# Feature tile padded to 68 columns, low part of the fc2 product padded to 36 rows, and new engine orders in a two-layer attention kernel

## The reference

```
norm_X = layernorm(ctx) ; norm_F = layernorm(L0 output)
attended = softmax(norm_F @ norm_X.T / 16) @ norm_X
h = gelu(attended @ fc1_w.T + fc1_b)            # 4 features
cross = h @ fc2_w.T + fc2_b
self_att = softmax(norm_cross @ norm_cross.T / 16) @ norm_cross
out = norm_F + gamma2 * (cross + gamma1 * self_att)
```

## Time and profile before

| what | value |
|---|---|
| median of 3 runs | 1124.83 us (1122.71 to 1127.54) |
| the profiled execution's own time | 1123.86 us |
| its span, first to last instruction | 1122.1 us |
| mean granted TensorE clock | 0.945 of full |
| busy: PE / weight loads / DVE / ACT / POOL | 999.5 / 820.9 / 672.6 / 623.4 / 249.0 us |

### The profile page before, as it was taken

One profiled execution on the slowest core, in us unless ns is written; L12 is line 12 of the kernel. 1 busy time (PEld: TensorE's weight loads), 2 busy tenths in 40 slices (PEclk: granted clock), 3 DMA queues, 4 the chain that ended last, 5 costly groups with the idle time before them and its releaser, 6 DMA issues.

```text
span 1122.1 us, 22714 instructions
## 1 busy us (share of the span) xinstructions
PE 999.5 (89%) x8556; PEld 820.9 (73%) x8556; DVE 672.6 (60%) x1509; ACT 623.4 (56%) x1318; POOL 249.0 (22%) x306
## 2 busy tenths in 40 slices
PE   2576889899999999999999999999999999989764
PEld 1455677778788787878787787878887878777652
DVE  3624364758576675758485856667575848565542
ACT  4243446474756665665647465756567574845332
POOL 4000011112213131413132221213141312231332
PEclk9676789999999999999999999999999999999975
DMA  5221202110211212121112112121212111110000
GB/s 172 93 77 38 82 24 69 65 53 33 69 61 58 73 48 81 47 74 49 54 47 75 39 58 72 49 82 48 82 48 67 53 52 43 50 37 17 10 10 9
DMA packets 68868, 63.65 MB, mean 57 GB/s; under 512 B 17156, under 2 KB 64173, under 8 KB 68784
## 3 DMA queue, kind: packets, MB, share of 16 engines
q1 hardware_dynamic: 68784, 62.50, 17.3%
HBM read 16.18 MB, written 4.19 MB: 18 GB/s over the span
## 4 chain that ended last, share of the span: by engine, by line
PE 71%; DVE 13%; ACT 6%; issue 6%; DMA 2%; POOL 1%; SPq 1%; ACTq 0%; DVEq 0%; POOLq 0%
PE mring L928 16%; PE ring L928 15%; PE down_ps L1071 7%; PE od L1021 7%; DVE mx_sa L773 6%; PE ring L1007 5%; PE ring L987 4%; PE mring L1135 3%; PE ring L1033 2%; ACT probs L631 2%; PE ring L936 2%; PE mring L1081 2%; PE ring L1041 1%; PE mring L1098 1%; DVE xn_a L746 1%
## 5 line engine op out<-in xcount | busy, mean ns | idle before, releaser
L631 ACT ACTIVATE probs<-ring 128x1024 f32<-128x1024 f32 (+1 forms) x192 | 190.6, 1023 | 24.0 <-PE ring L1007 22.3
L502 POOL TENSOR_TENSOR hidT_lo<-hid,hidT_hi 128x256 fp32r<-128x256 f32 x128 | 93.9, 739 | 457.4 <-ACT hidT_hi L660 457.4
L773 DVE TENSOR_REDUCE mx_sa<-ring 128x4 f32<-128x1024 f32 x128 | 152.8, 1219 | 14.8 <-PE ring L987 14.8
L815 DVE SCALAR_TENSOR_TENSOR hid<-hid,mring 128x256 f32<-128x256 f32 x128 | 53.1, 415 | 84.9 <-ACT hid L652 84.8
L778 DVE TENSOR_REDUCE mx_ca<-ring 128x4 f32<-128x308 f32 x128 | 55.4, 475 | 78.2 <-PE ring L987 77.4
L652 ACT ACTIVATE hid<-mring 128x256 f32<-128x256 f32 x128 | 48.7, 380 | 83.2 <-PE mring L928 83.2
L987 PE MATMUL ring<-pk_sa 63*128 63x256 f32 x512 | 67.9, 347 | 27.7 <-DVE mx_sa L773 15.7
L987 PEld LDWEIGHTS ring<-pk_sa 63*128 63x128 f32 x512 | 41.3, 199 | 51.2 <-DVE mx_sa L773 16.0
L1071 PE MATMUL down_ps<-down_hi,hidT_hi 128*128 128x256 f32 x256 | 77.2, 302 | 0.0
L1021 PE MATMUL od<-probs,vz_sa 128*32 128x256 f32 x1024 | 76.8, 400 | 0.1
L1071 PE MATMUL down_ps<-down_lo,hidT_hi 128*128 128x256 f32 x256 | 72.5, 283 | 0.0
(11 more groups left out here) (235 smaller groups left out, 2645.0 us busy)
## 6 DMA issues: line engine op xcount, KB each, us to landing
pk_sa<-qkT SPq DMA_DIRECT2D x96, 256.0 KB, 2.6
qpk_ca<-qkT SPq DMA_DIRECT2D x48, 256.0 KB, 2.6
x_sb<-x SPq DMA_DIRECT2D x16, 256.0 KB, 2.7
x_res<-x SPq DMA_DIRECT2D x16, 256.0 KB, 2.9
out<-o_sb SPq DMA_DIRECT2D x16, 256.0 KB, 2.2
kpk_ca<-qkT SPq DMA_DIRECT2D x48, 78.0 KB, 2.3
ctx_sb<-ctx SPq DMA_DIRECT2D x16, 77.0 KB
ctx_l<-ctx SPq DMA_DIRECT2D x16, 77.0 KB
```

The source lines that it names most:

```text
L502: nc.gpsimd.tensor_tensor(hidT[1][:, m % HID, :], hid[:, m % 2, :], hidT[0][:, m % HID, :].bitcast(F32), ALU.subtract).then_inc(S["hidlo"] ...
L631: nc.scalar.activation(granule(g, tag)[0:rows_, i0:i0 + 2, :, :].rearrange("p i h t -> p h i t"), ring_tile(("E", tag, k))[0:rows_].rearra ...
L773: nc.vector.tensor_reduce(mx[tag][:, :, :, k].rearrange("p q h -> p h q"), ps[:].rearrange("p h (q t) -> p h q t", t=T), AX_X, ALU.max).th ...
L815: nc.vector.scalar_tensor_tensor(out=hid[:, m % 2, :], in0=hid[:, m % 2, :], scalar=1.0, in1=ps[:, 0:T], op0=ALU.add, op1=ALU.mult).then_i ...
```

## The change

`fc2_lo` gets the 36 rows of `fc2_hi`, its added rows zero, and the low product of `f2` runs over all 36 rows of `g_r`. `xf` gets 68 columns (`HALF + FC`, 64 + 4), the last 64 zero, and `h4` writes 68 PSUM rows, of which four are read as before. DVE clears both tiles once at the start; PE and DVE wait for five instead of three such fills. The five lists in `ORDER` are replaced; the same steps stand in them.

```
-        fc2_lo = sb("fc2_lo", [FC + 1, D], F32R)
+        fc2_lo = sb("fc2_lo", [LO_AT + FC, D], F32R)
-        xf = sb("xf", [SKV, FC])
+        xf = sb("xf", [SKV, HALF + FC])
...
-                nc.scalar.activation(xf[:], mring_tile(("sc",))[...], ACT.Copy)
+                nc.scalar.activation(xf[:, 0:FC], mring_tile(("sc",))[...], ACT.Copy)
...
+            nc.vector.memset(fc2_lo[:].bitcast(F32), 0.0).then_inc(s_vset, 1)
+            nc.vector.memset(xf[:], 0.0).then_inc(s_vset, 1)
+            dve.wait_ge(s_vset, 5)
...
-            nc.vector.tensor_tensor(fc2_lo[:], ...)
+            nc.vector.tensor_tensor(fc2_lo[0:FC + 1], ...)
...
-            pe.wait_ge(s_vset, 3)
+            pe.wait_ge(s_vset, 5)
...
-                mm(ps[0:FC, 0:T], xf[:], lpT, start=True, stop=True)
+                mm(ps[0:HALF + FC, 0:T], xf[:], lpT, start=True, stop=True)
...
-                    last = mm(ps[...], g_r[0:FC + 1, q * P:(q + 1) * P], fc2_lo[:], ...)
+                    last = mm(ps[...], g_r[:, q * P:(q + 1) * P], fc2_lo[:], ...)
```

The list of PE before and after:

```
-        dnp.2@-2 qk.sa@1 dnp.3@-2 dnp.4@-2 E.ca.0@-1 pv.sa.3@0 E.ca.1@-1 E.ca.2@-1 gu.7@-2 nCT@-3 oT.sa@0 E.ca.3@-1 pv.ca.0@-1 s2@-3 cT.ca@0 aT.sa@0
-        pv.ca.1@-1 v.ca@0 nXT@-2 oT.ca@-1 wo.sa@0 dnp.5@-2 S.sa.0@1 aT.ca@-1 dnp.6@-2 dnp.7@-2 S.sa.1@1 wo.ca@-1 S.sa.2@1 p2T@-3 S.sa.3@1 S.sa.4@1 pv2@-3
-        S.sa.5@1 T.mlp@-1 v.sa@1 S.sa.6@1 S.sa.7@1 gu.0@-1 T.ca@0 gu.1@-1 maxT.sa@1 qk.ca@0 gu.2@-1 dnp.0@-1 E.sa.0@1 E.sa.1@1 gu.3@-1 nFT@-2 E.sa.2@1
-        E.sa.3@1 pv.sa.0@1 sc@-2 E.sa.4@1 gu.4@-1 E.sa.5@1 S.ca.0@0 pv.sa.1@1 gu.5@-1 S.ca.1@0 E.sa.6@1 dnp.1@-1 pT@-2 E.sa.7@1 S.ca.2@0 h4@-2 pv.sa.2@1
-        S.ca.3@0 T.sa@2 gu.6@-1 maxT.ca@0 f2@-2
+        qk.sa@1 pv.sa.2@0 pv.sa.3@0 E.ca.0@-1 E.ca.1@-1 gu.7@-2 oT.sa@0 E.ca.2@-1 pv.ca.0@-1 nCT@-3 cT.ca@0 aT.sa@0 dnp.4@-2 E.ca.3@-1 dnp.5@-2 wo.sa@0
+        S.sa.0@1 pv.ca.1@-1 v.ca@0 oT.ca@-1 s2@-3 aT.ca@-1 S.sa.1@1 dnp.6@-2 dnp.7@-2 wo.ca@-1 S.sa.2@1 p2T@-3 S.sa.3@1 nXT@-2 S.sa.4@1 pv2@-3 S.sa.5@1 v.sa@1
+        T.mlp@-1 S.sa.6@1 S.sa.7@1 gu.0@-1 T.ca@0 gu.1@-1 maxT.sa@1 qk.ca@0 gu.2@-1 E.sa.0@1 E.sa.1@1 gu.3@-1 nFT@-2 dnp.0@-1 E.sa.2@1 E.sa.3@1 pv.sa.0@1
+        sc@-2 E.sa.4@1 E.sa.5@1 pv.sa.1@1 gu.4@-1 E.sa.6@1 S.ca.0@0 gu.5@-1 S.ca.1@0 E.sa.7@1 dnp.1@-1 pT@-2 S.ca.2@0 S.ca.3@0 h4@-2 gu.6@-1 T.sa@2 dnp.2@-1
+        maxT.ca@0 dnp.3@-1 f2@-2
```

The other lists, cut to the places that the prediction speaks of (ACT; DVE's last words):

```
- act   hi.5@-2 E.ca.0@-1 o.sa.1@0 E.ca.1@-1 E.ca.2@-1 gu.7@-2
+ act   E.ca.1@-1 E.ca.2@-1 gu.7@-2 cT.ca@0 aT.sa@0 o.ca.0@-1
...
- act   norm.mlp@-1 h1@0 norm.ca@0 T.mlp@-1 v.sa@1 gu.0@-1 ws.7@2 T.ca@0 ws.10@1
+ act   norm.mlp@-1 h1@0 norm.ca@0 nXT@-2 ws.5@3 T.mlp@-1 v.sa@1 gu.0@-1 T.ca@0
...
- act   f2@-2 gu.6@-1 qk.sa@2
+ act   f2@-2 ws.6@3 gu.6@-1 qk.sa@2 o.sa.1@1 E.ca.0@0 ws.0@6
- dve   T.sa@1 ws.2@4 lnstat.nc@-3 gu.6@-2 qk.sa@1 ... ws.8@1 oT.ca@-1 ws.9@1 ... maxsplit.sa@1 ... ws.10@1
+ dve   T.sa@1 lncen.nx@-2 lnstat.nc@-3 qk.sa@1 gu.6@-2 ... maxsplit.sa@1 ... ws.9@1 ... ws.10@1 scn@-2 S.ca.0@0 ws.8@2
```

More of the change, by code:

```diff
@@ L49 @@
     "sp": """
-        wl.10@1 ldr@0 wl.2@5 ldcl@-1 wl.4@4 pqk.sa.1@1 mr.sa@1 pq.ca@0 wl.9@2 pk.ca@0 wl.0@6 st@-3 wl.5@3 wl.1@6 mr.ca@0 ldx@3 pqk.sa.0@2 ldc@1 wl.6@3 wl.7@3
-        wl.8@3 wl.3@5
+        wl.2@5 pqk.sa.1@1 wl.6@4 wl.7@4 ldr@1 wl.8@4 ldc@1 mr.sa@1 ldcl@-1 wl.9@3 pq.ca@0 wl.0@6 pk.ca@0 st@-3 mr.ca@0 ldx@3 wl.1@6 wl.3@5 wl.4@5 pqk.sa.0@2
+        wl.5@5 wl.10@2
     """,
     "pool": """
-        lnstat.nc@-2 hi.5@-1 hi.6@-1 hi.7@-1 ms.mlp@0 ms.ca@1 bF@-2 hi.0@0 lnstat.nf@-1 hi.1@0 bC@-2 hi.2@0 ms.sa@3 hi.3@0 lnstat.nx@0 hi.4@0
+        hi.2@-1 hi.3@-1 hi.4@-1 lnstat.nx@-1 lnstat.nc@-2 hi.5@-1 hi.6@-1 hi.7@-1 bF@-2 ms.mlp@0 ms.ca@1 lnstat.nf@-1 hi.0@0 ms.sa@3 hi.1@0 bC@-2
@@ L60 @@
-        gu.5@-1 o.sa.0@1 E.sa.6@1 pT@-2 E.sa.7@1 hi.4@-1 ws.8@2 h4@-2 T.sa@2 maxT.ca@0 f2@-2 gu.6@-1 qk.sa@2
+        E.ca.1@-1 E.ca.2@-1 gu.7@-2 cT.ca@0 aT.sa@0 o.ca.0@-1 E.ca.3@-1 nCT@-3 ws.2@4 ws.7@2 o.ca.1@-1 hi.6@-2 v.ca@0 hi.7@-2 aT.ca@-1 ws.9@1 s2e@-3 p2T@-3
+        ws.10@1 norm.mlp@-1 h1@0 norm.ca@0 nXT@-2 ws.5@3 T.mlp@-1 v.sa@1 gu.0@-1 T.ca@0 norm.sa@2 maxT.sa@1 hi.0@-1 gu.1@-1 qk.ca@0 hi.1@-1 gu.2@-1 ws.8@2
+        E.sa.0@1 ws.3@4 E.sa.1@1 gu.3@-1 nFT@-2 E.sa.2@1 hi.2@-1 E.sa.3@1 hi.3@-1 E.sa.4@1 E.sa.5@1 sce@-2 gu.4@-1 E.sa.6@1 o.sa.0@1 ws.1@5 gu.5@-1 E.sa.7@1
@@ L61 @@
+        pT@-2 h4@-2 T.sa@2 maxT.ca@0 hi.4@-1 ws.4@4 hi.5@-1 f2@-2 ws.6@3 gu.6@-1 qk.sa@2 o.sa.1@1 E.ca.0@0 ws.0@6
     """,
     "dve": """
-        maxsplit.ca@-1 glo@-3 ws.6@2 T.sa@1 ws.2@4 lnstat.nc@-3 gu.6@-2 qk.sa@1 lncen.nc@-3 lncen.nx@-2 ws.3@4 gu.7@-2 oT.sa@0 cT.ca@0 aT.sa@0 ws.4@4 s2@-3
-        ws.8@1 oT.ca@-1 ws.9@1 wo.sa@0 p2T@-3 ws.0@5 S.sa.0@1 aT.ca@-1 dn@-2 S.sa.1@1 wo.ca@-1 S.sa.2@1 S.sa.3@1 ms.mlp@-1 S.sa.4@1 xn.mlp@-1 ms.ca@0 pv2@-3
-        S.sa.5@1 ws.5@4 T.mlp@-1 xn.ca@0 S.sa.6@1 S.sa.7@1 maxsplit.sa@1 T.ca@0 gu.0@-1 lnstat.nf@-2 gu.1@-1 qk.ca@0 lncen.nf@-2 ws.10@1 gu.2@-1 gu.3@-1
@@ L66 @@
-        lnstat.nx@-1 out@-3 ms.sa@2 sc@-2 S.ca.0@0 scn@-2 ws.7@2 gu.4@-1 S.ca.1@0 gu.5@-1 ws.1@5 xn.sa@2 S.ca.2@0 S.ca.3@0
+        T.sa@1 lncen.nx@-2 lnstat.nc@-3 qk.sa@1 gu.6@-2 lncen.nc@-3 ws.5@3 oT.sa@0 cT.ca@0 aT.sa@0 gu.7@-2 wo.sa@0 S.sa.0@1 oT.ca@-1 s2@-3 aT.ca@-1 S.sa.1@1
+        dn@-2 p2T@-3 wo.ca@-1 S.sa.2@1 S.sa.3@1 ws.2@4 ms.mlp@-1 S.sa.4@1 xn.mlp@-1 ms.ca@0 pv2@-3 S.sa.5@1 xn.ca@0 T.mlp@-1 S.sa.6@1 S.sa.7@1 ws.6@2
+        maxsplit.sa@1 T.ca@0 gu.0@-1 ms.sa@2 ws.9@1 lnstat.nf@-2 gu.1@-1 ws.7@2 qk.ca@0 lncen.nf@-2 ws.0@6 ws.1@6 gu.2@-1 xn.sa@2 ws.3@4 gu.3@-1 out@-3 sc@-2
@@ L67 @@
+        lnstat.nx@-1 ws.10@1 scn@-2 S.ca.0@0 ws.8@2 gu.4@-1 S.ca.1@0 gu.5@-1 S.ca.2@0 S.ca.3@0 maxsplit.ca@0 glo@-2 ws.4@4
     """,
     "pe": """
[L69 to L71 removed]
@@ L686, in sce @@
                                          bias=lnm[:, q:q + 1], scale=L1_SCALE, accum_out=lsum[:, q:q + 1]).then_inc(S["lp"].sem, 1)
-                nc.scalar.activation(xf[:], mring_tile(("sc",))[0:SKV, QT * SKV:QT * SKV + FC], ACT.Copy).then_inc(S["xf"].sem, 1)
+                nc.scalar.activation(xf[:, 0:FC], mring_tile(("sc",))[0:SKV, QT * SKV:QT * SKV + FC], ACT.Copy).then_inc(S["xf"].sem, 1)
             def h4(n):
@@ L1113, in h4 @@
                 ps = mfill(n, "h4")
-                mm(ps[0:FC, 0:T], xf[:], lpT, start=True, stop=True).then_inc(S["h4"].sem, 1)
+                mm(ps[0:HALF + FC, 0:T], xf[:], lpT, start=True, stop=True).then_inc(S["h4"].sem, 1)
             def f2(n):
@@ L1122, in f2 @@
                     mm(ps[:, q * D:(q + 1) * D], g_r[:, q * P:(q + 1) * P], fc2_hi[:], start=True, stop=False)
-                    last = mm(ps[:, q * D:(q + 1) * D], g_r[0:FC + 1, q * P:(q + 1) * P], fc2_lo[:], start=False, stop=True)
+                    last = mm(ps[:, q * D:(q + 1) * D], g_r[:, q * P:(q + 1) * P], fc2_lo[:], start=False, stop=True)
                 last.then_inc(S["f2"].sem, 1)
```

5 lines of the change are left out of this document (1 added, 4 removed).

## The result

The changed kernel takes **1130.07 us** in the median of 20 runs (1123.16 to 1135.36); the kernel before, in 20 runs beside it, 1123.36 us (1121.68 to 1127.54). The ratio is 1.0055, 95% interval 1.0037 to 1.0073: slower by a little more than 0.5%. I had forecast 1120 us, range 1109 to 1129, and gave "slower" 0.10.

The account below looks back on a forecast made before the run. The prediction took PE's own issue, 59.3 of 61.0 us per item, to bound the middle, with single chains deciding start and end. Middle -5.3, start +3.6 and end -2.3 gave -4.0 on 1123.86: 1119.9 us, range 1109 to 1129.

Parts of the forecast that it names:

- slower: Whole kernel: slower by over 0.5%, above 1129.5 us; chance 0.10.
- The waits: PE's waits in the middle: 1.66 us per item before, 1.7 to 1.8 after, +0.05; bounds -0.7 and +0.7.
- Two places: PE's waits: oT.sa for E.ca.0's exp, 0.7 us; S.sa.7 for v.sa's copy behind T.mlp's, 0.9 us per item.
- Middle: Item 0 to item 12: -0.57 + 0.08 + 0.05 = -0.44 us per item, times 12: -5.3 us.
- The rival with ACT's in-order queue as the bound: At T.mlp and v.sa, S.sa.7 waits for a copy behind another copy; slower, 1127.5 us; chance 0.14.
- f2: f2's four matmuls, all with 36 rows, cost 0.67 us instead of 1.24: -0.57 us per item.
- h4 and the changes of shape: h4, moved and padded to 68 columns: +0.08 us per item; PE's array-shape changes elsewhere, 37 before and after: 0.
- The 0.22 that I put for each fp32 pass of `h4`: h4 at 68 columns, in gu.6's full-array shape, pays two plain fp32 passes of 0.22 us.
- The start: First turns: DVE's reordered low parts delay item 0 by 2.0 us and the first exp further; +3.6 us, bounds 0 and +7.
- The end: Items 13 to 15 and last turn: f2's gain of 1.5 us, about 0.8 from earlier gu.7; -2.3 us, bounds -5 and +2.
- The sign that I had named: Last turn: gu.7 of the last item starts early, up to 2.6 us before its 1069.49.

Follow-up runs that it names:

- c_three: Changed kernel with three moves on PE: dnp.0 ahead of E.sa.0, dnp.4 ahead of oT.sa, T.mlp ahead of v.sa; 1109.35 us, ratio 0.9865.
- b_f2: Kernel before, with its orders and 4-column xf, only fc2_lo padded to 36 rows; 1113.77 us, ratio 0.9914.
- look_1: Changed kernel itself, unaltered, profiled once more; 1135.13 us.
- look_2: Changed kernel itself, unaltered, a further single profile; 1129.61 us.
- look_3: Changed kernel itself, unaltered, a further single profile; 1130.49 us.

## Why the prediction was wrong

**The waits: the step that failed.** "I moved the steps by their durations. Two places matter." There were three. The two that I named came about as worked out: `oT.sa` waits 0.79 for the exp (predicted 0.7), `S.sa.7` 0.74 for `v.sa`'s copy (up to 0.93). With `S.sa.4` (0.24) they come to 1.77 us, inside my 1.7 to 1.8, though the parts that I listed (0.7, 0.1, 0.9 and 0.3, less the 0.15 that the view doesn't name) add up to 1.85. `nFT` was not looked at, because PE's list has it behind `gu.3` before and after; that its neighbour `dnp.0` had left was 0.48 us of wait, and 0.57 per item when undone, some 7 us of the run. My sum for the waits was +0.05 us per item, the measured change is +0.59. Middle: -5.3 predicted, +1.8 measured. The rival with ACT's in-order queue as the bound came out on the right side for another reason than its own. Its pair, `T.mlp` and `v.sa` (0.50 us when undone), was in my sum as well; what it added, that `T.ca` and `S.sa.4` give nothing back, did not come: the wait of `T.ca` is gone and that of `S.sa.4` went from 0.52 to 0.24.

**f2.** -0.57 predicted, -0.56 measured with it alone. The four starts and the exit came out to 0.01 us.

**h4 and the changes of shape.** Predicted +0.08 and 0. PE's time without waits fell by 0.44 us per item, of which 0.56 to 0.58 are `f2`'s, so the two together cost 0.12 to 0.14. The direction was right too: with 4 columns the new orders are 0.14 worse. The 0.22 that I put for each fp32 pass of `h4` stands in no row of before; in the changed kernel's first profile its two passes start at 667.04 and 667.31 us, and `gu.6` at 667.34.

**The start.** +3.6 predicted; +4.5 in the first profile, between +0.4 and +5.8 over the five of the changed kernel, +3.2 in their mean. The delay of item 0 is shown: +1.8 for the low part of `T.sa` (predicted 2.0), first exp 61.0 (61.8), and 3.9 us in the median when both are undone in `c_three`. At the granted clock of before, 0.83 up to `f2`, it is +4.5 and +5.8; the two early starts, at 0.86, nearly hide it. That the forecast lies so near the mean is in part luck, since it had no term for the clock.

**The end.** -2.3 predicted, with bounds of -5 and +2. It is -5.2 and -4.0 us where the stretch is missing and +3.6 where it is there. The sign that I had named is there, `gu.7` of the last item early. PE's timeline in the first profile:

```profile
1071.10 0.51 PE L931 MATMUL mring<-hT_m_hi,gate_hi 128*128 128x256 f32 x2 [0.69 <-ACT l_buf L667]
```

That is 94.7 us behind `f2` of item 12; before it was 99.4, in `b_f2` 97.4. But the clock between the two is 1.00 here, 0.97 before and 0.96 in `b_f2`, so how much of the gain is the order's is not shown. `b_f2`, with the orders of before, has an end of 148.2 already.

By the groups the stretch is there in 22 of 32 runs (the 19 of the two slower groups, `look_1`, `look_2` and `look_3`): 22/32 x 7.6 to 8.8 us = 5 to 6 us on the mean. My sum had no term for the clock, and I had not asked what the pauses in the turn at 1000 us would do to it. Middle and start leave the ten runs of the lowest group 0.2% above the kernel before; this term makes it 0.55%.

The sum was -4.0 us and the median lies 6.7 above that of before, so 10.7 us went astray. The middle is 7.1 of them (5.8 to 7 with `nFT`); the start, in the mean of its five profiles, gives 0.4 back; the end, weighted by the groups, is +1.0 us instead of -2.3, 3.3 more: 5 to 6 us for the stretch, less the 2 to 3 by which the end without it beats the forecast. This is an estimate, from five profiles and the three groups; it leaves 0.7 us open.
